# Attention on TensorE: value products of two key tiles in one group at each fourth step, in place of one tile at each second

## The reference, cut to what matters

```
b, s, _ = hidden_states.shape                    # 8, 512; H = 16 heads of 16
q = shape(hidden_states @ Wq.T)                  # hidden_states = layernorm(x)
k = shape(hidden_states @ Wk.T)
v = shape(hidden_states @ Wv.T)
position_bias = compute_bias(rel_emb, s, s)
scores = einsum('bhqd,bhkd->bhqk', q, k) * SCALING + position_bias
attn = softmax(scores, axis=-1)
ctx = einsum('bhqk,bhkd->bhqd', attn, v)
return ctx @ Wo.T
```

## Time and profile before

| | |
|---|---|
| runs | 854.51, 849.15, 852.29 us; median 852.29 |
| profiled execution | 849.1 us, span 847.3 us, mean granted clock 0.95 |
| stage `project` | until about 103 us of the span |
| stage `attend` | until about 525 us; products of scores alone before 128 us |
| stage `finish` | the rest |
| PE, DVE, ACT, POOL busy | 777.7, 615.5, 477.7, 258.3 us |

### The profile page before, as it was taken

How to read it: one execution, slowest core, us unless ns; L and a number is a source line. 1 busy time by engine, 2 the same in 40 slices (tenths; PEclk the granted TensorE clock), 3 DMA queues, 4 the chain that set the end, 5 groups by cost and what they waited for, 6 DMA issues and landing times. The chain is left out here.

```text
span 847.3 us, 18113 instructions
## 1 busy us (share of the span) xinstructions
PE 777.7 (92%) x6177; PEld 539.9 (64%) x6177; DVE 615.5 (73%) x1907; ACT 477.7 (56%) x720; POOL 258.3 (30%) x405
## 2 busy tenths in 40 slices
PE   4999889999999999999999997788888799999994
PEld 2777647666666666666665653565654499999952
DVE  4666487888888888888887871476675367777646
ACT  2444305666666666666666675264564177777720
POOL 1112111111211211121111120257676336666710
PEclk9999956999999999999999999798997989999998
DMA  4999894444455434543354553545432645555379
GB/s 117 271 340 359 276 238 105 127 119 117 120 147 144 121 104 131 153 143 97 102 160 136 174 173 143 129 151 198 168 109 82 174 131 153 168 159 162 115 260 366
DMA packets 74486, 140.73 MB, mean 166 GB/s; under 512 B 14504, under 2 KB 34624, under 8 KB 74222
## 3 DMA queue, kind: packets, MB, share of 16 engines
q1 hardware_dynamic: 62818, 116.90, 45.5%
q0 software_dynamic: 9792, 19.54, 7.0%
q10 hardware_dynamic: 1788, 3.18, 1.2%
HBM read 85.70 MB, written 56.78 MB: 168 GB/s over the span
## 5 line engine op out<-in xcount | busy, mean ns | idle before, releaser
L731 DVE CUSTOM_DVE_ANT_0 sums<-pS,near 128x512 bf16<-128x512 f32 x512 | 329.4, 687 | 52.5 <-PE pS L797 44.1
L764 ACT ACTIVATE prob<-pE 128x1024 f32<-128x1024 f32 x256 | 248.6, 1022 | 152.9 <-PE pE L822 152.8
L822 PEld LDWEIGHTS pE<-bandT,place 64*128 64x128 f32 x2048 | 169.3, 192 | 12.3
L822 PE MATMUL pE<-bandT,place 64*128 64x244 f32 (+2 forms) x2048 | 166.3, 274 | 0.0
L797 PE MATMUL pS<-k_st,q_st 48*128 48x512 f32 x512 | 139.9, 478 | 7.1 <-DMA k_st<-k_parts 4.1
L797 PEld LDWEIGHTS pS<-k_st,q_st 48*128 48x128 f32 x512 | 63.6, 194 | 117.5 <-DVE nmax L731 90.0
L836 PE MATMUL pC<-prob,v_aug 128*32 128x512 f32 x1024 | 136.6, 608 | 1.0 <-ACT ctx_sb L772 1.0
L814 PE MATMUL pE<-q_st,k_st 62*128 62x512 f32 x512 | 117.1, 408 | 2.0 <-issue 2.0
L1088 POOL DMA_INDIRECT expert_rows<-rb,xr x76 | 83.8, 1103 | 59.5 <-DVE rb L1266 47.6
L1072 POOL DMA_INDIRECT routed_rows<-xr,slot_i x64 | 64.4, 1006 | 31.3 <-issue 18.9
L814 PEld LDWEIGHTS pE<-q_st,k_st 62*128 62x128 f32 x512 | 58.6, 191 | 8.5 <-ACT prob L764 5.0
(11 more groups left out here) (180 smaller groups left out, 1032.3 us busy)
## 6 DMA issues: line engine op xcount, KB each, us to landing
xr<-routed_rows SPq DMA_DIRECT2D x38, 258.0 KB, 2.9
q_st<-q_parts SPq DMA_DIRECT2D x64, 128.0 KB, 2.7
k_st<-k_parts SPq DMA_DIRECT2D x64, 128.0 KB, 2.9
ctx<-ctx_sb SPq DMA_DIRECT2D x32, 256.0 KB, 2.8
q_parts<-qk SPq DMA_DIRECT2D x14, 512.0 KB, 7.9
k_parts<-qk SPq DMA_DIRECT2D x14, 512.0 KB, 7.3
near<-bias_by_distance SPq DMA_DIRECT2D x16, 448.0 KB, 5.4
xr<-expert_rows SPq DMA_DIRECT2D x12, 512.0 KB, 7.7
```

Of the source, the lines that this page charges most:

```text
L731: dve.tensor_tensor_reduce(sums[:, r % 4], pS[:, unit % PS], near[:, hg % 2, j, lead:lead + S], -1.0, BIG, ALU.add, ALU.min, nmax[:, j, t: ...
L764: act.activation(prob[:, par, 2 * step:2 * step + 2], pE[:, 2 * (step % 2):2 * (step % 2) + 2], ACT.Exp).then_inc(exp_done, 1)
L822: ins = pe.matmul(pE[:, bank + side, a:z], place[rows, half], bandT[rows, (quad // 2) % 2, pair, part, lead:lead + z - a], start=False, st ...
```

## The change

PE's order within a slot is rewritten. A slot is two turns of four steps. Within a turn, with S for scores, E for exponents and V for the values of one key tile, the order was S E, E S V, S E, E S V. It is now S E E S E S E S V V: all four steps of scores and exponents first, alternating after the second, and then the two key tiles 2 turn and 2 turn + 1 one after the other. The steps themselves, their waits and signals, and the lists of all other engines are the same.

```diff
--- before.py
+++ after.py
@@ -838,16 +838,26 @@
                     ins.then_inc(pv_done, 1)
 
                 def slot(n, u, quad, first=False, last=False):
-                    for step in range(STEPS):
+
+                    def ahead_of(step):
                         ahead, other = divmod(STEPS + step + LEAD, STEPS)
-                        early = step % 2 == 0
-                        if early and not (last and u + ahead > 3):
+                        if not (last and u + ahead > 3):
                             scores(n + ahead, (u + ahead) % 4, quad + 1 + (u + ahead) // 4, other)
-                        exponents(n, u, step, quad, u, first and u == 0)
-                        if not early and not (last and u + ahead > 3):
-                            scores(n + ahead, (u + ahead) % 4, quad + 1 + (u + ahead) // 4, other)
-                        if step % 2 == 1 and not (first and u == 0):
-                            values(n - 1, (u + 1) % 2, step // 2, first and u == 1)
+
+                    fresh = first and u == 0
+                    for turn in range(2):
+                        step = 4 * turn
+                        ahead_of(step)
+                        exponents(n, u, step, quad, u, fresh)
+                        exponents(n, u, step + 1, quad, u, fresh)
+                        ahead_of(step + 1)
+                        exponents(n, u, step + 2, quad, u, fresh)
+                        ahead_of(step + 2)
+                        exponents(n, u, step + 3, quad, u, fresh)
+                        ahead_of(step + 3)
+                        if not fresh:
+                            for t in (2 * turn, 2 * turn + 1):
+                                values(n - 1, (u + 1) % 2, t, first and u == 1)
 
                 for step in range(STEPS + LEAD):
                     scores(step // STEPS, step // STEPS, 1, step % STEPS)
```

## The result

The changed kernel takes 876.15 us (median of six runs, 874.46 to 880.53). The kernel before took 853.4 us over its six runs beside it. The ratio is 1.0274, with a 95% interval of 1.024 to 1.0308: slower by 22.8 us. 882 was forecast, 29 to 30 more than before, with a range of 871 to 896; the direction and the range held, the size was some 7 us too large.

A forecast was written before the change was run, and what follows sets the result against it. PE's own stream was taken to bound attention. Full slots 29.3 us, last two slots 2.4, less credits of 0.8 and 1.0, gave 29.9 more: 852.3 + 29.9 = 882 us, range 871 to 896 at 80% or a little more.

The forecast's parts named there:

- What bounds the kernel: Attention slots: the order of PE's own stream sets the pace, 12.24 us a slot, with DVE at 10.85 and ACT at 8.34.
- The saved passages: Each attention turn: fewer passages between V and its neighbours; if nothing waited, 5.70 us against 6.12, 0.42 less.
- A weight load in the additional passages from S to E: Two additional S-to-E passages a turn: by the skill's rule some 0.11 us each, turn 5.92; the sum leaves it out.
- The two latencies: Each turn: third E waits 0.47 us for the first exponential; the last S's second side waits for DVE's reduction.
- The bound S to S: Three score banks: one S to the next takes at least 1.31 us, where the new order wants 0.91 for two distances.
- The sum: Whole kernel: 29.3 for full slots, plus 2.4 for the last two, less 0.8 and 1.0, gives 29.9 us more.
- the two credits: Time given back: 0.8 us from the first slot's idle PE and 1.0 us from late maxima near 446 us.
- the last two slots: Slots with almost no S: a turn of 5.12 us becomes 5.73, 0.61 more; four such turns, 2.4 us.
- The second credit: First slot, without V and at half clock: E between two S covers a wait for DVE, at most 0.8 us less.
- (a): Rival: in attention the waits do not bite and only saved passages remain, 24 us less, 828 us; chance 0.04.
- (b): Rival: the exponential's latency bites but DVE's does not, 12.36 us a slot, 856 us; chance 0.04.
- (c): Rival: stalls in attention make PE's clock fall, one turn in eight cold, 36 us more, 918 us; chance 0.06.

The follow-up runs named there:

- e4: Kernel before, with the exponential over half its columns and DVE's maxima over 128 of 512 keys: 846.03 us, ratio 0.9882.
- e3: Changed kernel, with the exponential over half its columns and DVE's maxima over 128 of 512 keys: 831.86 us, ratio 0.9776.
- e1: Changed kernel, with only the exponential cut to half its columns: 874.05 us, ratio to before 1.0254.
- e2: Changed kernel, with only DVE's maxima cut to 128 of the 512 keys: 849.69 us, ratio to before 0.9979.
- the second pair: Kernel before and changed kernel, each profiled once more without edits: one time each, 859.02 and 878.06 us.
- e11: Kernel before, unedited, run once more for a second profile: 859.02 us.
- e6: Changed kernel, with all four key tiles of values moved to the slot's end: 901.47 us, ratio to before 1.0592.
- e8: Kernel before, with the maxima's transposition moved between the next item's first and second unit, except items 0, 1 and 31: 848.24 us, ratio 0.9971.
- e5: Changed kernel, keeping grouped values but otherwise the order of before, S E E S S E E S V V: 897.86 us, ratio to before 1.0545.
- e9: Kernel before, with the four late loads of x issued one per slot instead of two in each of two slots: 852.26 us, ratio 0.9997.
- e10: Kernel before, with both the later transposition of e8 and the spread x loads of e9: 850.58 us, ratio 0.9986.
- e7: Kernel before, with the maxima's transposition one step later, after the next item's first two units, maxima in two buffers: 856.46 us, ratio 1.0068.

## Why the prediction was right, and where its size was off

**What bounds the kernel.** Held. e4 takes over half of DVE's and 0.4 of ACT's durations away from the order of before and gains 0.13 us a slot: PE's stream was the bound, and the only other time in it the wait behind DVE's turn.

**The saved passages.** Forecast 0.42 us a turn against the mean of before, of which 0.07 is the turn's wait; e4 against e3 measures 0.30. e3's turn is 5.76 rather than 5.70, since even an exponential of 0.60 us holds the third E a little: in the turn from 263.26 us its load stands 1.87 us behind the first S load, where the forecast without waits has 1.93 - 0.11 = 1.82. V V at 1.86 us held to the hundredth.

**A weight load in the additional passages from S to E.** By the rule of the Trainium skill that the prediction weighs ("TensorE: Matmul & The Clock Gate", section "The mechanism", a load overlaps a running matmul only where the row groups differ) a turn without waits would have been 5.92, and e3's is 5.76, so the rows were the better guide. The same section of the Trainium skill also lets a load into the background weight buffer go ahead of matmuls in flight, which is what e3 agrees with.

**The two latencies.** Held within 0.02 us at each of five points of the half, and so did the order in which they matter. That it adds their charges, 0.47 us for the third E and 0.39 or 0.50 for the last S, is right for the two together: 1.83 a slot, and e3 takes 1.71 from it. What it does not say is what would be left of the loss if only one of them went. e1 and e2 show that: the first alone can go without gain, the second not. The bound S to S of 1.31 us held (331.55 - 330.24 in the loads above); in e1, where the third E no longer spaces the S, it is 1.22.

**The sum.** This is where the step failed that was mis-sized: the two credits, 1.0 us for the late maxima and 0.8 for the first slot. The full slots from the first to the last but two copies came to 28 intervals of 13.24 - 12.26 = 0.98, 27.4 us (forecast 1.01 each), the last two slots to 11.58 + 11.33 - 10.56 - 10.16 = 2.2 (forecast 2.4). With slot 1 at 1.0 that is 30.6 (forecast 31.7), so these terms held.

The late maxima gave back more than 1.0. From first to last copy the first pair of profiles differs by 26.1, not by 27.4 + 2.2 = 29.6, so 3.5 us were given back; the second pair differs by 24.2, so there it is 5.4. The stop of PE at that place, in the changed kernel:

```profile
466.17 0.19 PEld L797 LDWEIGHTS pS<-k_st,q_st 48*128 48x128 f32 x2 [0.84 <-DVE nmax L731]
466.81 0.22 PEld L814 LDWEIGHTS pE<-q_st,k_st 62*128 62x128 f32 x2 [0.45 <-issue]
```

is 0.64 - 0.11 = 0.5 us of weight load behind S, where before's, ended at 449.40 after an S load at 446.89, was 449.40 - 446.89 - 0.11 = 2.4:

```profile
449.40 0.22 PEld L814 LDWEIGHTS pE<-q_st,k_st 62*128 62x128 f32 x2 [2.33 <-issue]
```

e11 has a second one of 2.3 us, ended at 488.60. The half clock behind before's stop, which the credit did not price, did not happen. A longer slot alone does not explain this: e6, with slots of 13.88 us, has a wait of 1.9 us near 527 us. Nor does the length of a stop settle whether the clock falls. Behind e11's stop at 488 us it fell, behind a slightly longer one of e8 it did not:

```profile
489.00:492.00 3.00, 3.00 (x26) 2.34 (x26) 0.35 (x1) 1.74 (x2) 0.70 (x1) 0.50 1.04 356
```

```profile
440.59 0.22 PEld L821 LDWEIGHTS pE<-q_st,k_st 62*128 62x128 f32 x2 [2.28 <-issue]
```

```profile
441.00:445.00 4.00, 4.00 (x52) 2.77 (x48) 2.45 (x8) 2.29 (x3) 0.70 (x1) 1.00 0.71 181
```

The second credit, 0.8 us for the first slot, was too small too. The first copy came 4.3 us earlier in the first pair of profiles and 3.8 in the second, though slot 1 ahead of it was itself 1 us longer: 5.3 and 4.8 us. Of these, 1.7 and 0.5 are an earlier start of attention, which the change does not touch, so at most 3.6 and 4.3 can be the change's. Full clock by 127 us in place of 137 to 141 goes with it. Whether the order causes it is open: of the profiles with the order of before in the first slot (e4, e5, e8, e9, e10) the half clock lasted 27.3, 23.9, 20.5, 27.3 and 20.5 us, in the two of the unchanged kernel 34.1 and 30.7 (and 41.0 in e7), in the six with the new order 20.5 to 27.3.

Together 8.8 and 10.2 us came back ahead of the last copy, not 1.8: 30.6 less these is 21.8 and 20.4, and 22.8 (20.5 to 26.3) was measured. That the total came out 7 us below the forecast is thus the credits' doing for the most part; how much of them the change itself causes stays open. The first profiled pair differs by 27.8 only because the stage after attention was 6.0 us shorter in the first profile of before.

**The rivals.** (a), no wait bites, fell by the 0.5 us in front of each third E. (b) fell by DVE's waits, and e2 shows it at the 12.36 us a slot where it would have been. (c), a falling clock, fell: the changed kernel's attention has no drop at all between 127 us and its end. Two gaps of some 0.2 to 0.5 us in every 6.6 leave the granted clock at 1.00. The Trainium skill, "TensorE: Matmul & The Clock Gate", section "A second HAM failure mode: psum-queue depth-cycling", tells of a bf16 kernel whose frequent micro-idles made the clock oscillate; this trace does not show that.

## What to carry to other kernels

A piece of work that depends on nothing near it, as the value products here, is also the cover for the round trips of its neighbours: before grouping such pieces, write down each ring (PSUM banks, producer, consumer, release) and the least time from one use to the next, and see whether the new order leaves it. Where two such waits stand in one loop, removing the one that the profile shows first can give nothing (e1): take both away together in an experiment, or price them one by one against the pair. And before crediting one order with a shorter stop for a late transfer, profile the same kernel twice: here the unchanged kernel had one such stop of over 2 us in one profile and two in the other.

## What was not expected of the hardware

- Half clock for 20.5 to 41.0 us at the head of attention, in fourteen profiles of much the same work there. In the windows above PE is busy 12.5 of 14 us at a clock of 0.52 or 0.63, and 13.2 of 14 at 1.00. With the stage after attention (322 to 331 us in all profiles) it is where the profiles scatter; away from late maxima the slots of either kernel repeat within 0.07 us.
- The release of one engine by another is regular: 0.06 us from ACT's or DVE's end to PE's weight load at each of the waits worked out here and in the prediction.
- Moving the transposition by 0.5 us (e8) or by 1.2 us (e7) did the same between the first and the last copy: slots of 12.1 us, and waits of 6.2 and 6.3 us for late maxima from 200 to 500 us, where the two profiles of the unchanged order have 2.6 and 4.4. Both suggest that the round trip of the maxima through DRAM has less than half a microsecond to spare in some slots.
